# Causal blocks of 64 rows, two heads side by side in one score tile, other products in four bursts per slot

## The chip, the core and the metric

The program runs on one core of a Trainium2 chip. Its engines work at the same time and meet only at semaphores: the PE (TensorE, the matrix product, which loads a stationary operand, the weights, and streams a moving one past it into PSUM), DVE (VectorE), ACT (ScalarE), POOL (GpSimd) and SP (SyncE, here the one that issues all transfers). The metric is the time of one execution on the device in microseconds, as the median of several runs. A profile shows one such execution.

## What is computed

Each of 32 sequences of 256 rows and 128 columns is normalised by rows (xn). The result is x + attention(xn) + experts(xn):

```python
scores = jnp.einsum('bhqd,bhkd->bhqk', q, k) / math.sqrt(hd)
causal = jnp.tril(jnp.ones((s, s), bool))
scores = jnp.where(causal, scores, -jnp.inf)
attn = jax.nn.softmax(scores, axis=-1)
out = jnp.einsum('bhqk,bhkd->bhqd', attn, v)
out = out.transpose(0, 2, 1, 3).reshape(b, s, d)
return out @ Wo.T + bo
...
logits = jnp.einsum('btd,ed->bte', x, gate_w)
top_val, top_idx = jax.lax.top_k(logits, top_k)
top_w = jax.nn.softmax(top_val, axis=-1)
y_all = jnp.einsum('btd,edm->btem', x, We)
x_experts = jnp.take_along_axis(y_all, top_idx[..., None], axis=2)
out = jnp.sum(x_experts * top_w[..., None], axis=2)
```

There are 16 heads of 8 columns, and two of 8 experts are kept for each row. All products are wanted to single precision.

## The kernel before

q and k are each split into three bf16 parts and stacked, with a causal mask written as further rows, so that one bf16 product over up to 123 rows gives a masked score to single precision (qstack and kstack, made by way of DRAM). A score is computed twice. The first pass (score_item, tile score_ps) has queries in the partitions; DVE takes the negated row maximum (take_max, into negmax). The maxima are transposed (pe_mT), split in two bf16 parts (mT, on ACT and DVE) and loaded by SP into two more rows of qstack. The second pass (scoreT_item, tile scoreT_ps) has keys in the partitions and gives scores less the maximum, of which ACT takes the exponential (take_exp, into probs). The values (values) then multiply probs by vaug, which holds v and a column of ones for the sum, in four column tiles of 32, one head in each; the result oT_ps is copied by ACT (oT), transposed (pe_o), divided on DVE (rden, o_sb), transposed again (pe_oTn), copied by ACT (oTn) and multiplied by Wo (pe_y); DVE adds the rest and SP stores it.

A tile holds 512 columns. Only blocks on or below the diagonal are computed, in blocks of 128 rows: of four, three. So a pass has 12 items of 4 matmuls of 128 columns, 3 items for each group of 4 heads. score_ps and scoreT_ps have two buffers each: item n + 2 of a pass waits on the PE until DVE (or ACT) has done with item n.

The other products of the PE: turn_input (transposes of xn, from which ACT and DVE make xnT and its two halves, copy_input, halve_input, round_input), project (q and k of a later sequence, into m2, which part1 on ACT and take_rest on DVE read), values and gates (pe_vg, into m1, read by take_values on ACT), and experts (four products of 512 columns, three passes each, into m1 for DVE, lower_experts, and m2 for ACT, upper_experts).

The order is written out by hand. Each engine has a function slot(t, s), called once for each slot s by over_slots; in it a loop over the items n, with the pieces of other work placed at an n. In slot s the scores are of sequence s, the turned scores of s-1 and s-2 (behind, with LAG items between), the experts of s-1, the values and what follows of s-2, the projections of s+2, the input of s+3. Each engine works through its own list, so an instruction that waits holds up what stands behind it in that list. There are 34 slots. What stands around the change on ACT is this:

```python
if n == 6 and has(s, -2):
    act.wait_ge(pe_pv, upto(fin, per=NG))
    act.wait_ge(pe_o, upto(fin + (-1)))
    a.copy(oT[:].rearrange("p r t -> p (r t)"), oT_ps[:]).then_inc(act_oT, 1)
...
f, k = behind(t, s, n)
if f:
    take_exp(f, k)
```

## Time and profile before

| | |
|---|---|
| three runs | 515.61, 516.22, 518.01 us; median 516.22 |
| profiled execution | span 510.5 us from its first to its last instruction; its time with what lies around the span is not listed apart |
| PE busy | 477.8 us, 94% of the span, 6274 instructions |
| DVE busy | 420.7 us, 82%, 1111 instructions |
| ACT busy | 396.9 us, 78%, 1062 instructions |
| POOL busy | 345.9 us, 68%, 561 instructions |
| DMA | 67.8 MB, 133 GB/s |
| chain that ended last | PE 89%, DVE 3%, ACT 3%, DMA 2% |

A busy share is the union of the instructions' times on an engine. Matmuls overlap in their pipeline: one of 128 columns lasts some 0.22 us in the trace, but the next starts after a quarter of that, so what the PE spends on a group is read from the start of the group to the start of the next. In the rows of the timeline neighbours of one kind are merged, with their count (x4) and the time from the first's start to the last's end.

### The profile page before, as it was taken

What the parts mean: (1) busy time and instruction counts of PE and PEld (TensorE: products, weight loads), DVE (VectorE), ACT (ScalarE), POOL (GpSimd) and SP (SyncE); (2) the same over time, 40 slices, a digit from 0 to 9 for tenths busy, and PEclk for the clock granted to TensorE, in tenths of its full rate; (3) what the DMA queues carried; (4) which work ended last, traced back from release to release, by engine and by line L of the source; (5) the groups of instructions that cost most, each with busy time, mean ns of one, the idle gap of its engine ahead of it and who ended that gap; (6) DMA issues with size and microseconds to landing.
All of it is one profiled execution on the core that took longest, in us unless ns stands there. A gap on an engine that the chain in (4) does not pass through costs nothing.

```text
span 510.5 us, 17312 instructions
## 1 busy us (share of the span) xinstructions
PE 477.8 (94%) x6274; PEld 393.8 (77%) x6274; DVE 420.7 (82%) x1111; ACT 396.9 (78%) x1062; POOL 345.9 (68%) x561
## 2 busy tenths in 40 slices
PE   2548799999999999999999999999999999999995
PEld 1437688888888888888888888888888888888863
DVE  5897698888888898888888898888888898888721
ACT  3644688888888888888888888888888888887773
POOL 7264657777777777778777777777777777755443
PEclk9999999999999999999999999999999999999999
DMA  4664746656547566655465566655556566552000
GB/s 124 195 140 117 188 122 152 161 136 156 134 119 162 130 151 156 160 139 145 105 168 128 148 154 160 156 141 143 139 128 147 138 152 161 133 132 44 15 13 22
DMA packets 64281, 67.79 MB, mean 133 GB/s; under 512 B 6828, under 2 KB 59180, under 8 KB 59484
## 3 DMA queue, kind: packets, MB, share of 16 engines
q1 hardware_dynamic: 64196, 66.68, 53.0%
q8 instruction: 50, 0.82, 0.7%
q14 instruction: 35, 0.29, 0.2%
HBM read 44.90 MB, written 21.23 MB: 130 GB/s over the span
## 4 chain that ended last, share of the span: by engine, by line
PE 89%; DVE 3%; ACT 3%; DMA 2%; issue 2%; SPq 0%; POOL 0%; DVEq 0%; POOLq 0%; ACTq 0%
PE m L841 23%; PE oT_ps L911 17%; PE scoreT_ps L887 13%; PE score_ps L867 12%; PE scoreT_ps L892 5%; PE score_ps L861 5%; PE m L953 3%; PE m L996 3%; PE m L1014 3%; PE m L926 2%; PE m L1021 1%; PE m L962 1%; DMA qstack<-mT 1%; ACT probs L499 1%; DVE negmax L625 1%
## 5 line engine op out<-in xcount | busy, mean ns | idle before, releaser
L625 DVE TENSOR_REDUCE negmax<-score_ps 128x2 f32<-128x512 f32 (+1 forms) x384 | 249.7, 678 | 46.4 <-PE score_ps L867 43.7
L499 ACT ACTIVATE probs<-scoreT_ps 128x512 f32<-128x512 f32 x384 | 216.5, 603 | 74.2 <-PE scoreT_ps L887 48.0
L394 POOL TENSOR_TENSOR fours<-lower,upper 128x512 f32<-128x512 f32 x64 | 81.7, 1276 | 54.1 <-ACT upper L549 54.1
L841 PE MATMUL m<-we_hl,xnT_hl 128*128 128x512 f32 x384 | 114.6, 420 | 0.0
L867 PE MATMUL score_ps<-kstack,qstack 72*128 72x128 bf16 (+1 forms) x1024 | 103.8, 224 | 5.6 <-DVE negmax L625 5.5
L887 PE MATMUL scoreT_ps<-qstack,kstack 123*128 123x128 bf16 (+1 forms) x1024 | 102.0, 221 | 3.3 <-DMA qstack<-mT 2.6
L911 PE MATMUL oT_ps<-probs,vaug 128*32 128x256 f32 (+1 forms) x2048 | 96.7, 329 | 0.2 <-ACT probs L499 0.2
L887 PEld LDWEIGHTS scoreT_ps<-qstack,kstack 123*128 123x128 bf16 (+1 forms) x1024 | 68.1, 98 | 26.5 <-ACT probs L499 15.4
L911 PEld LDWEIGHTS oT_ps<-probs,vaug 128*32 128x32 f32 x2048 | 57.3, 109 | 29.1 <-ACT probs L499 0.4
L549 ACT ACTIVATE upper<-m,weight 128x128 f32<-128x128 f32 x256 | 73.1, 376 | 8.2 <-PE m L841 8.2
L867 PEld LDWEIGHTS score_ps<-kstack,qstack 72*128 72x128 bf16 (+1 forms) x1024 | 72.1, 100 | 8.8 <-DVE negmax L625 7.6
L841 PEld LDWEIGHTS m<-we_hl,xnT_hl 128*128 128x128 f32 x384 | 65.8, 192 | 8.9
L371 POOL TENSOR_TENSOR parts<-rest,parts 128x256 bf16<-128x256 f32 x60 | 40.1, 690 | 35.2 <-ACT parts L528 35.2
L861 PE MATMUL score_ps<-kstack,qstack 123*128 123x128 bf16 x512 | 51.1, 223 | 2.4 <-DVE negmax L625 1.4
L361 POOL TENSOR_SCALAR xn<-x_sb,mv,rstd 128x128 f32<-128x128 f32 x58 | 46.4, 806 | 7.4 <-POOL rstd L353 7.4
L892 PE MATMUL scoreT_ps<-qstack,kstack 123*128 123x128 bf16 x512 | 50.1, 220 | 0.7 <-ACT probs L499 0.7
L662 DVE TENSOR_TENSOR lower<-m,weight 128x512 f32<-128x512 f32 x64 | 43.5, 679 | 2.6 <-PE m L841 2.6
L433 POOL TENSOR_TENSOR pairs<-fours 128x512 f32<-128x512 f32 x32 | 40.7, 1272 | 2.5
L892 PEld LDWEIGHTS scoreT_ps<-qstack,kstack 123*128 123x128 bf16 x512 | 31.8, 98 | 11.2 <-issue 8.7
L861 PEld LDWEIGHTS score_ps<-kstack,qstack 123*128 123x128 bf16 x512 | 35.3, 99 | 3.3 <-DVE negmax L625 2.0
L841 PE MATMUL m<-xnT_hl,wqk_hl 128*128 128x256 f32 x192 | 33.3, 314 | 4.1 <-DVE xnT_hl L678 4.1
L841 PEld LDWEIGHTS m<-xnT_hl,wqk_hl 128*128 128x128 f32 x192 | 27.3, 207 | 5.6 <-issue 4.9
(81 smaller groups left out, 649.7 us busy)
## 6 DMA issues: line engine op xcount, KB each, us to landing
kstack<-scratch SPq DMA_DIRECT2D x93, 192.0 KB
scratch<-parts SPq DMA_DIRECT2D x64, 192.0 KB, 2.4
qstack<-scratch SPq DMA_DIRECT2D x62, 192.0 KB
qstack<-scratch SPq DMA_DIRECT2D x31, 256.0 KB
x_sb<-in_x SPq DMA_DIRECT2D x32, 128.0 KB, 2.3
scratch<-parts SPq DMA_DIRECT2D x32, 128.0 KB, 1.9
out<-out_sb SPq DMA_DIRECT2D x32, 128.0 KB, 3.7
qstack<-mT SPq DMA_DIRECT2D x64, 8.0 KB, 2.1
```

The source lines that it names most:

```text
L361: ins = g.tensor_scalar(xn[:, q, :], x_sb[nxt.buf][:, q, :], mv[:, q, 0:1], rstd[:, q:q + 1], ALU.subtract, ALU.mult)
L394: g.tensor_tensor(fours[:, :, q, :], lower[:, :, q, :], upper[:, :, q, :], ALU.add).then_inc(pool_sum, 1)
L499: a.activation(o, i, ACT.Exp, scale=SCALE).then_inc(act_exp, 1)
L549: ins = a.activation(upper[:, e, q, :], m2[:, e * D:(e + 1) * D], ACT.Copy, scale=weight[m.buf][:, q, EH + e:EH + e + 1])
L625: v.tensor_reduce(o, score_ps[n % 2][:].rearrange("p (h k) -> p h k", h=w), axis=AX.X, op=ALU.max, negate=True).then_inc(dve_max, 1)
L662: v.tensor_tensor(lower[:, :, q, :], m1[:].rearrange("p (e m) -> p e m", e=EH), weight[m.buf][:, q, 0:EH].unsqueeze(2).to_broadcast([P, EH ...
L841: ins = tn.matmul(o, l, r, start=first, stop=l is low)
L861: ins = tn.matmul(ps[:, c * P:(c + 1) * P], qs[0:ALL_ROWS, h, 0:P], ks[0:ALL_ROWS, h, 0:P], start=True, stop=True)
L867: ins = tn.matmul(ps[:, c * S + q * P:c * S + (q + 1) * P], qs[0:top, h, P:S], ks[0:top, h, q * P:(q + 1) * P], start=True, stop=True)
L887: ins = tn.matmul(ps[:, c * S + q * P:c * S + (q + 1) * P], ks[0:top, h, 0:P], qs[0:top, h, q * P:(q + 1) * P], start=True, stop=True)
L892: ins = tn.matmul(ps[:, c * P:(c + 1) * P], ks[0:ALL_ROWS, h, P:S], qs[0:ALL_ROWS, h, P:S], start=True, stop=True)
L911: ins = tn.matmul(o, va[:, q, h, :], i, start=q == 0 and grp % VGRP == 0, stop=q == 1 and grp % VGRP == VGRP - 1, skip_group_check=True)
```

## The change

Scores, turned scores and values go by blocks of 64 rows: of 16 blocks 10 lie on or below the diagonal. The array is used as two column tiles of 64: head h goes to PSUM partitions 0 to 63 and head h + 8 to 64 to 127 of the same tile, by two matmuls with stationary operands of 64 columns, one behind the other. An item of 512 columns then holds blocks of two or four such pairs. A pass has 10 items in two sets of five kinds: `low` (two pairs, three steps each of 64, 128 and 64 columns), `mid` (four pairs, one step of 128) and `top` (two pairs, two steps of 128). The row maxima of `low` items come out in parts, and a small reduction on DVE folds them (fold_max). vaug holds keys of two heads in the upper and lower partitions, with the two heads' values in different columns, so one matmul of the values serves both; the values come in two bursts of 16. Values and gates and the output product go in two column tiles too.

The order is new on all engines. On the PE the other products stand at four places of a slot: two transposes of o_sb, that of negmax, project and values and gates at n = 1; values and half the experts at n = 3; the same at n = 6; transposes of oT and of the input at n = 8. The end of a sequence (the second transposes, output product, store) moves a slot later, and there are 35 slots. The maxima's rows are loaded by four transfers and not two.

```diff
--- before.py
+++ after.py
...
-HG = 4
-NG = H // HG
-ITEMS = 3 * NG
+BLK = HALF
+NBLK = S // BLK
+NPAIR = H // 2
+SETS = 2
+QUADS = NPAIR // SETS
+KINDS = 5
+ITEMS = SETS * KINDS
...
+def score_tables():
+
+
+    low = [[(c, (c % 2) * S, 0, ALL_ROWS, 0, 1), (c, (c % 2) * S + BLK, 2, MAX_ROW, 0, 2),
+            (c, (c % 2) * S + 3 * BLK, 2, ALL_ROWS, 2, 3)] for c in range(QUADS)]
+    mid = [(c, c * P, 1, ALL_ROWS, 0, 2) for c in range(QUADS)]
+    top = [[(c, (c % 2) * S, 3, MAX_ROW, 0, 2), (c, (c % 2) * S + P, 3, ALL_ROWS, 2, 4)] for c in range(QUADS)]
+    return [low[0] + low[1], low[2] + low[3], mid, top[0] + top[1], top[2] + top[3]]
...
+    mid = [(c, c * P, 2, ALL_ROWS, 2, 4) for c in range(QUADS)]
...
+
+SCORES, SCORES_T = score_tables(), turned_tables()
+PROBS = {(c, blk): (kind, col) for c in range(QUADS) for blk, kind, col in
+         ((0, c // 2, (c % 2) * S), (1, 3 + c // 2, (c % 2) * S), (2, 2, c * P), (3, 3 + c // 2, (c % 2) * S + 3 * BLK))}
 
 
 def stand_alone(eng, passed):
...
                     m = t + (-1)
 
                     sp.wait_ge(dve_mT, upto(m))
                     for part in range(MAX_PARTS):
-                        sp.dma_start(qstack[m.buf][MAX_ROW + part:MAX_ROW + part + 1], mT[:, part]).then_inc(dma_max, 16)
+                        for half in range(2):
+                            row = qstack[m.buf][MAX_ROW + part:MAX_ROW + part + 1, half * NPAIR:(half + 1) * NPAIR]
+                            sp.dma_start(row.rearrange("r c (i t) -> r (c i) t", i=NBLK),
+                                         mT[:, part, half * HALF:(half + 1) * HALF]).then_inc(dma_max, 16)
                 if s == 1:
...
+                if has(s, -3):
+                    store(t + (-3))
...
-                pr = probs[grp]
+                group, kind = k // KINDS, k % KINDS
                 act.wait_ge(pe_scoreT, upto(f, per=ITEMS, k=k + 1))
...
-                    o = pr[:, 1]
-                    i = scoreT_ps[k % 2][:].rearrange("p (h q) -> p h q", h=HG)
-                a.activation(o, i, ACT.Exp, scale=SCALE).then_inc(act_exp, 1)
+                if kind == 0:
+                    act.wait_ge(pe_pv, upto(f + (-1), per=SETS, k=group + 1))
+                a.activation(probs[group][:, kind], scoreT_ps[k % 2][:], ACT.Exp, scale=SCALE).then_inc(act_exp, 1)
...
+                    f, k = behind(t, s, n)
+                    if n == 1 and has(s, -1):
+                        act.wait_ge(pe_mT, upto(mix))
+                        act.wait_ge(dma_max, upto(mix + (-1), per=MAX_LOADS, unit=16))
+                        a.copy(mT[:, 0], oT_ps[0:NPAIR * NBLK, 0:P]).then_inc(act_mT, 1)
...
-                    if n == 6 and has(s, -2):
-                        act.wait_ge(pe_pv, upto(fin, per=NG))
+                    if n == 3 and has(s, -3):
+                        act.wait_ge(pe_oTn, upto(last))
+                        act.wait_ge(pe_y, upto(last + (-1)))
+                        a.copy(oTn[:], m0[:, 0:S]).then_inc(act_oTn, 1)
+                    if n == 7 and has(s, -2):
+                        act.wait_ge(pe_pv, upto(fin, per=SETS))
                         act.wait_ge(pe_o, upto(fin + (-1)))
                         a.copy(oT[:].rearrange("p r t -> p (r t)"), oT_ps[:]).then_inc(act_oT, 1)
-                    if n == 11 and has(s, NXT):
-                        copy_input(t + NXT)
-                    if n == 11 and has(s, -1):
-                        upper_experts(mix, 1)
-                    if n == 11 and has(s, NXT):
-                        round_input(t + NXT)
-                    f, k = behind(t, s, n)
                     if f:
                         take_exp(f, k)
...
+                    if n in (4, 5) and has(s, -1):
+                        upper_experts(mix, 0, range(2 * (n - 4), 2 * (n - 3)))
+                    if n in (7, 8) and has(s, -1):
+                        upper_experts(mix, 1, range(2 * (n - 7), 2 * (n - 6)))
+                    if n == 8 and has(s, NXT):
+                        copy_input(t + NXT)
+                    if n == 9 and has(s, NXT):
+                        round_input(t + NXT)
...
+                nm, ps = negmax[t.buf], score_ps[n % 2][:]
+                first, kind = QUADS * (n // KINDS), n % KINDS
+                some = slice(first + 2 * (kind % 2), first + 2 * (kind % 2) + 2)
+                if kind < 2:
+                    o, i = nm[:, :, some, 0].rearrange("p g c -> p c g"), ps.rearrange("p (c g k) -> p c g k", c=2, g=NBLK)
+                elif kind == 2:
...
+            def fold_max(t):
+
+                nm = negmax[t.buf]
+                dve.wait_ge(dve_max, upto(t, per=ITEMS, k=KINDS + 2))
+                v.tensor_reduce(nm[:, 0, :, 2], nm[:, 1:NBLK, :, 0].rearrange("p g c -> p c g"),
+                                axis=AX.X, op=ALU.min).then_inc(dve_fold, 1)
...
+                    if n == 3 and has(s, 0):
+                        best_numbers(t)
+                    if n == 4 and has(s, -1):
+                        lower_experts(mix, 0)
...
+                    if n == 7 and has(s, -1):
+                        lower_experts(mix, 1)
+                    if n == 7 and has(s, 0):
+                        fold_max(t)
...
+                for pair, col, blk, top, k0, k1 in SCORES[n % KINDS]:
+                    for half in range(2):
+                        h = head(QUADS * (n // KINDS) + pair, half)
+                        ins = tn.matmul(ps[half * HALF:(half + 1) * HALF, col:col + (k1 - k0) * BLK],
+                                        qs[0:top, h, blk * BLK:(blk + 1) * BLK], ks[0:top, h, k0 * BLK:k1 * BLK],
                                         start=True, stop=True)
...
+                for pair, col, blk, top, q0, q1 in SCORES_T[n % KINDS]:
+                    for half in range(2):
+                        h = head(QUADS * (n // KINDS) + pair, half)
+                        ins = tn.matmul(ps[half * HALF:(half + 1) * HALF, col:col + (q1 - q0) * BLK],
+                                        ks[0:top, h, blk * BLK:(blk + 1) * BLK], qs[0:top, h, q0 * BLK:q1 * BLK],
                                         start=True, stop=True)
...
-                        o = oT_ps[quad, c0:c0 + S] if q == 0 else oT_ps[quad, c0 + P:c0 + S]
-                        i = pr[:, 0:3:2, c, :] if q == 0 else pr[:, 1, c, :]
-                        ins = tn.matmul(o, va[:, q, h, :], i, start=q == 0 and grp % VGRP == 0,
-                                        stop=q == 1 and grp % VGRP == VGRP - 1, skip_group_check=True)
+                    pe.wait_ge(dve_mT, upto(f + 1) if f.n + 1 < NSEQ else upto(f))
+                for blk in range(NBLK):
+                    for c in range(QUADS):
+                        kind, col = PROBS[c, blk]
+                        ins = tn.matmul(oT_ps[VW * c:VW * (c + 1), group * S + blk * BLK:(group + 1) * S],
+                                        vaug[f.buf][:, blk, QUADS * group + c, :],
+                                        probs[group][:, kind, col:col + S - blk * BLK],
+                                        start=blk == 0, stop=blk == NBLK - 1, skip_group_check=True)
...
+            def values_and_gates(t, s):
...
+                for blk in range(NBLK):
+                    for half in range(2):
+                        skip = 0 if blk % 2 == half else E
+                        ins = tn.matmul(m1[half * HALF:(half + 1) * HALF, blk * GV + skip:(blk + 1) * GV],
+                                        xnT[t.buf][:, blk * BLK:(blk + 1) * BLK], wvg_sb[:, half * GV + skip:(half + 1) * GV],
+                                        start=True, stop=True)
+                ins.then_inc(pe_vg, 1)
...
+                    if n == 1 and has(s, -3):
...
+                            ins = tn.transpose(m0[:, q * P:(q + 1) * P], o_sb[:, q].rearrange("p j c d -> p (j c d)"), ident[:])
+                        ins.then_inc(pe_oTn, 1)
...
+                        pe.wait_ge(dve_fold, upto(mix))
+                        pe.wait_ge(act_oT, upto(last))
+                        tn.transpose(oT_ps[0:NPAIR * NBLK, 0:P], negmax[mix.buf][:, 0].rearrange("p c i -> p (c i)"),
+                                     ident[:]).then_inc(pe_mT, 1)
                     if n == 1 and has(s, PRE):
...
+                    if n == 1 and has(s, 0):
+                        values_and_gates(t, s)
                     if n == 3 and has(s, -2):
                         values(fin, 0)
-                        values(fin, 1)
-                    if n == 4 and has(s, -1):
+                    if n == 3 and has(s, -1):
                         if s == 1:
...
-                        experts(mix, 1)
+                        mix_experts(mix, s, 0)
+                    if n == 4 and has(s, -3):
+                        pe.wait_ge(act_oTn, upto(last))
+                        for blk in range(NBLK):
+                            half = blk % 2
+                            ins = tn.matmul(m0[half * HALF:(half + 1) * HALF, blk // 2 * P:(blk // 2 + 1) * P],
+                                            oTn[:, blk * BLK:(blk + 1) * BLK], wo_sb[:], start=True, stop=True)
+                        ins.then_inc(pe_y, 1)
                     if n == 6 and has(s, -2):
-                        values(fin, 2)
-                        values(fin, 3)
+                        values(fin, 1)
+                    if n == 6 and has(s, -1):
+                        mix_experts(mix, s, 1)
...
-                    if n == 9 and has(s, -1):
-                        pe.wait_ge(dve_lower, upto(mix, per=2, k=1))
-                        experts(mix, 2)
-                    if n == 11 and has(s, NXT):
...
-                        ins.then_inc(pe_y, 1)
                     if f:
                         scoreT_item(f, k)
```

How the instructions stand now is shown at three places. score_ps and scoreT_ps are the two passes' tiles, m0 to m2 the PSUM tiles of the other products. The first is the PE from the end of the second values of a slot to the transposes of oT. Before:

```order
L911 MATMUL oT_ps<-probs3,vaug0 32x256 x4
L911 MATMUL oT_ps<-probs3,vaug0 32x128 x4
L887 MATMUL scoreT_ps1<-qstack1,kstack1 128x128 x4
L867 MATMUL score_ps1<-kstack2,qstack2 128x128 x4
L892 MATMUL scoreT_ps0<-qstack1,kstack1 128x128 x4
L867 MATMUL score_ps0<-kstack2,qstack2 128x128 x4
L996 MATMUL m0<-ident,oT 128x128 x4
L887 MATMUL scoreT_ps1<-qstack1,kstack1 128x128 x4
L861 MATMUL score_ps1<-kstack2,qstack2 128x128 x4
L841 MATMUL m1<-we_hl,xnT_hl1 128x512 x3
```

After:

```order
L939 MATMUL oT_ps<-probs1,vaug2 32x128 x4
L939 MATMUL oT_ps<-probs1,vaug2 32x64 x4
L885 MATMUL m1<-we_hl,xnT_hl3 128x512 x3
L885 MATMUL m2<-we_hl,xnT_hl3 128x512 x3
L923 MATMUL scoreT_ps1<-qstack3,kstack3 64x128 x8
L904 MATMUL score_ps1<-kstack0,qstack0 64x128 x8
L923 MATMUL scoreT_ps0<-qstack3,kstack3 64x128 x8
L904 MATMUL score_ps0<-kstack0,qstack0 64x128 x8
L1049 MATMUL m0<-ident,oT 128x128 x4
L956 MATMUL m1<-ident,xn 128x128 x2
L923 MATMUL scoreT_ps1<-qstack3,kstack3 64x64 x2
L923 MATMUL scoreT_ps1<-qstack3,kstack3 64x128 x2
```

Four items (turned score, score, turned score, score) stand ahead of the transposes of oT as before, but now six matmuls of the experts stand between the values and the first of them. The second place is ACT at the same point of the slot. Before:

```order
L499 ACTIVATE probs0<-scoreT_ps0 128x2x2x128 [waits pe_pv,pe_scoreT]
L549 ACTIVATE upper<-m2,weight2 128x128 [waits pool_sum,pool_gate,pe_moe]
L549 ACTIVATE upper<-m2,weight2 128x128 x3
L567 COPY oT<-oT_ps 128x512 [waits pe_o,pe_pv]
L499 ACTIVATE probs0<-scoreT_ps1 128x2x2x128 [waits pe_scoreT]
L499 ACTIVATE probs0<-scoreT_ps0 128x512 [waits pe_scoreT]
L499 ACTIVATE probs1<-scoreT_ps1 128x2x2x128 [waits pe_pv,pe_scoreT]
```

After:

```order
L581 ACTIVATE upper<-m2,weight2 128x128 x2
L530 ACTIVATE probs0<-scoreT_ps1 128x512 [waits pe_scoreT]
L605 COPY oT<-oT_ps 128x512 [waits pe_o,pe_pv]
L530 ACTIVATE probs0<-scoreT_ps0 128x512 [waits pe_scoreT]
L581 ACTIVATE upper<-m2,weight2 128x128 [waits pool_sum,pool_gate,pe_moe]
L581 ACTIVATE upper<-m2,weight2 128x128
L530 ACTIVATE probs0<-scoreT_ps1 128x512 [waits pe_scoreT]
L581 ACTIVATE upper<-m2,weight2 128x128 x2
L568 COPY xnT2<-m1 128x256 [waits pe_xnT]
L530 ACTIVATE probs0<-scoreT_ps0 128x512 [waits pe_scoreT]
L573 CAST xnT_hl2<-xnT_high 128x256 [waits pe_moe,dve_halves]
L530 ACTIVATE probs1<-scoreT_ps1 128x512 [waits pe_pv,pe_scoreT]
```

The copy of oT stood ahead of the first exponential of the items that follow the values on the PE; now it stands behind it. The third place is the PE at the start of a slot, where project takes the halves of the input. Before:

```order
L887 MATMUL scoreT_ps1<-qstack1,kstack1 128x128 x4
L867 MATMUL score_ps1<-kstack3,qstack3 128x128 x4
L953 MATMUL m1<-wvg_sb,xnT3 128x136 x2
L962 MATMUL m0<-ident,negmax2 16x128 x2
L841 MATMUL m2<-xnT_hl1,wqk_hl 128x256 x6
L892 MATMUL scoreT_ps0<-qstack1,kstack1 128x128 x4
```

After:

```order
L904 MATMUL score_ps1<-kstack0,qstack0 64x64 x2
L1010 MATMUL m0<-ident,o_sb 128x128 x2
L1016 MATMUL oT_ps<-ident,negmax3 32x128
L885 MATMUL m2<-xnT_hl2,wqk_hl 128x256 x6
L979 MATMUL m1<-wvg_sb,xnT0 64x72
L979 MATMUL m1<-wvg_sb,xnT0 64x64 x2
L979 MATMUL m1<-wvg_sb,xnT0 64x72 x2
L979 MATMUL m1<-wvg_sb,xnT0 64x64 x2
L979 MATMUL m1<-wvg_sb,xnT0 64x72
L923 MATMUL scoreT_ps0<-qstack2,kstack2 64x128 x8
```

project has moved ahead of values and gates, and the second transposes (of o_sb) have come in front of it.

## Rows read from the trace of the kernel before

**Rows 1.** By stretch, twenty slots: us; busy us and count by engine; clock; DMA.
```profile
106.17:394.01 287.84, 287.84 (x3919) 240.94 (x3917) 252.67 (x680) 240.41 (x660) 213.09 (x341) 1.00 0.59 145
```

**Rows 2.** Waits of the PE, longest first: us in total, times, longest; first and last.
```profile
PE m L926 <- DVE xn L781: 8.2, 3, 6.2
...
PE m L996 <- ACT oT L567: 1.2, 2, 0.7
...
PE oT_ps L911 <- ACT probs L499: 0.2, 1, 0.2
```

**Rows 3.** Timeline, PE: start, us, engine, line, operation, tiles, count; a burst of values.
```profile
250.22 0.39 PE L887 MATMUL scoreT_ps<-qstack,kstack 123*128 123x128 bf16 x4
...
250.45 0.39 PE L861 MATMUL score_ps<-kstack,qstack 123*128 123x128 bf16 x4
...
250.77 1.51 PE L911 MATMUL oT_ps<-probs,vaug 128*32 128x256 f32 x32
...
252.21 0.41 PE L887 MATMUL scoreT_ps<-qstack,kstack 123*128 123x128 bf16 x4
```

**Rows 4.** By stretch, instructions on oT_ps alone: PE, PEld, ACT; clock; DMA.
```profile
250.70:250.80 0.10, 0.03 (x4) 0.03 (x5) 0.00 (x0) 1.00 0.95 251
```

**Rows 5.** Timeline, PE: the other products of a slot, with the groups behind them.
```profile
253.14 0.60 PE L996 MATMUL m<-ident,oT 128*128 128x128 f32 x4
...
253.59 0.40 PE L887 MATMUL scoreT_ps<-qstack,kstack 123*128 123x128 bf16 x4
...
258.30 0.68 PE L953 MATMUL m<-wvg_sb,xnT 128*128 128x136 f32 x4
...
258.82 0.38 PE L962 MATMUL m<-ident,negmax 128*16 128x128 f32 x2
...
258.95 0.96 PE L841 MATMUL m<-xnT_hl,wqk_hl 128*128 128x256 f32 x6
...
259.75 0.40 PE L892 MATMUL scoreT_ps<-qstack,kstack 123*128 123x128 bf16 x4
...
262.66 1.65 PE L841 MATMUL m<-we_hl,xnT_hl 128*128 128x512 f32 x6
...
264.14 0.40 PE L892 MATMUL scoreT_ps<-qstack,kstack 123*128 123x128 bf16 x4
```

**Rows 6.** Timeline: ACT, SP, and the two PE groups ahead of the third.
```profile
251.16 1.14 ACT L549 ACTIVATE upper<-m,weight 128x128 f32<-128x128 f32 x4
...
254.81 0.40 PE L887 MATMUL scoreT_ps<-qstack,kstack 123*128 123x128 bf16 x4
...
255.05 0.39 PE L867 MATMUL score_ps<-kstack,qstack 72*128 72x128 bf16 x4
...
255.25 1.09 ACT L499 ACTIVATE probs<-scoreT_ps 128x512 f32<-128x512 f32 x2 [0.63 <-PE scoreT_ps L887]
...
256.47 0.41 ACT L537 COPY xnT<-m 128x256 f32<-128x256 f32 x1
...
260.60 1.86 SPq L318 DMA_DIRECT2D qstack<-mT  x2
260.68 0.83 ACT L522 ACTIVATE parts<-m,bqk_sb 128x256 bf16<-128x256 f32 x2
...
263.15 0.70 ACT L528 CAST parts<-rest 128x256 bf16<-128x256 f32 x2
```

**Rows 7.** Timeline, DVE: the halves of the input, and rest.
```profile
257.02 0.42 DVE L674 TENSOR_SCALAR xnT_high<-m 128x256 uint32<-128x256 uint32 x1
...
257.47 0.42 DVE L678 TENSOR_TENSOR xnT_hl<-m,xnT_high 128x256 fp32r<-128x256 f32 x1
...
261.55 0.88 DVE L716 SCALAR_TENSOR_TENSOR rest<-m,bqk_sb,parts 128x256 f32<-128x256 f32 x2
```

**Rows 8.** Timeline, end of the program: a copy on ACT and who waited for it.
```profile
503.99 0.58 ACT L567 COPY oT<-oT_ps 128x512 f32<-128x512 f32 x1 [0.98 <-PE oT_ps L911]
...
504.63 0.66 PE L996 MATMUL m<-ident,oT 128*128 128x128 f32 x4 [0.71 <-ACT oT L567]
```

294 lines of the change are left out of this document (117 added, 177 removed).

## The prediction

> **What bounds the kernel now.** The first view is the table by stretches over twenty slots of the middle (a slot is one turn of the program's loop, on average one sequence). 287.84 us for twenty is 14.39 us a slot, and the PE is busy in all of it at the full granted clock of 1.00, while DVE works 12.63 us of a slot (252.67/20) and ACT 12.02 [rows 1]. Busy alone proves little for a pipelined engine, so the second view is the PE's waits: over the whole run they come to some 30 us in 14 rows, the longest from the start of the program, and the row that matters below, the PE waiting for ACT's copy of oT, stands there twice in 34 slots, 1.2 us together [rows 2]. So the PE never waits in the middle, and a slot lasts as long as the PE's stream of instructions. Work taken off DVE and ACT is worth nothing by itself. The third view is the PE's line of time, where the start of one group to the start of the next is its price: a score item of four matmuls of 128 columns costs 0.23 us, 0.058 a matmul (250.22 to 250.45) [rows 3].
>
> **What the change takes from the PE.** I write S0 to S9 and T0 to T9 for the new score and turned-score items (12 of each become 10).
> Scores: 96 matmuls of 128 columns (24 items, 5.5 us) become 96 steps of two matmuls each, one for each half of the array: 64 steps of 128 columns, 32 of 64. Do two column tiles run at the same time? In before the values run in four column tiles: four matmuls start inside a tenth of a microsecond, with at least as many weight loads [rows 4], so I take yes. A step of 128 columns then stays at 0.058. A step of 64 columns lies between its own columns, 0.033, and a weight load that hides no more: 128 columns of weights are loaded within a step of 0.11 (four steps in 0.45, 253.14 to 253.59) [rows 5], so 64 take at most about 0.058. I take 0.033, since in the nearest row, the values, the loads of a column tile hide behind the matmuls, and keep 0.058 for the range. Scores: 64 x 0.058 + 32 x 0.033 = 4.8 us, -0.7 (at 0.058: 5.6, no gain).
> The Trainium skill speaks against the change here: "TensorEngine Tiling (Array Packing)", Restrictions, says that column tiling switches Fast Weight Load off, and "TensorE: Matmul & The Clock Gate", LDWEIGHTS, puts a load without it at columns/1.2 ns, by which I estimate 53 ns for 64 columns. By that the upper end would hold, and the slot below would be 15.9 us, not 15.7; no row of before has a bf16 load in a column tile.
> Values: a burst of 32 instructions covers 768 columns (two groups of heads, 384 each) in each of four tiles and costs 1.44 us until the next group [rows 3]; a burst of one group in blocks of 64 covers 640. Less 0.10 for the way out, 1.34 x 5/6 = 1.12 us, twice a slot: -0.4.
> Between tilings the array seems to run empty: the item ahead of the values costs 0.32 and not 0.23 (250.45 to 250.77) [rows 3], so about 0.09 on the way in, and I take 0.10 on the way out. Before there are four such borders in a slot; now there are ten (one full-width burst ahead of the gates, values and experts twice, the transposes of oT and of the input). Six more: +0.6. Against it, the transposes of negmax, also in a 32-wide tile, follow full-width products with no gap (258.82, next 258.95) [rows 5], so zero is the lower bound.
> The Trainium skill states the same of a border ("TensorEngine Tiling", Key Properties: a change of mode drains the TensorE); the values agree, the negmax rows do not.
> The rest is equal within 0.1: experts 1.48 for six (262.66 to 264.14, less in two bursts of six than in three), project 0.80, values and gates 0.52, transposes of oT 0.45, each to the start of the next group [rows 5]; the output product, in half-width tiles, I put at 0.45 like these, one transpose of negmax at 0.1 where two stood.
> The PE's own sum: 4.8 + 2.24 + 2.96 + 0.80 + 0.53 + 0.45 + 0.45 + 0.23 + 0.22 + 0.1 + ten borders 0.96 = 13.7 us, 0.7 less than now.
>
> **What it adds: waits.** The other products now stand in four bursts. While the PE is in one, ACT and DVE run out of scores (each has two PSUM tiles); afterwards the PE waits for what they queued behind the next item. Prices: a score item on the PE reaches ACT 0.20 after the next group starts (255.05 to 255.25); two exponentials take 1.09, four experts' weightings 1.14, so two hold ACT 0.50, and I put the two vaug copies, of the same columns in all, at 0.52; two part1 take 0.83, part2 0.30 each [rows 6]. DVE: high to low 0.45, low 0.42; two rest 0.88 [rows 7]. ACT's copy of oT, of 512 columns like an exponential, lasts 0.58, and the PE starts 0.06 after its end (504.57 to 504.63) [rows 8]; so I take 0.58 for one exponential and 0.51 until ACT goes on. I go around one slot, from the end of T3; six-step items are 0.25 (four short steps), four-step items 0.23.
> A. The next project needs the input's halves. ACT: 0.20, exponential of T3 0.51, two weightings 0.50, copy of xnT 0.41 + 0.06; DVE: high 0.45, low 0.42 + 0.06: 2.61. The PE's S9, T4, S0, T5, S1, a border, three transposes: 1.6. It waits 1.0.
> B. project 0.80, border 0.10, gates 0.53: 4.04.
> C. The second half of the first experts' burst writes m2, which project filled, after rest has read it: 0.20 + logits 0.1 + vaug 0.52 + exponential 0.51 + part1 0.89 + rest 0.94 = 3.16, against 3.03 on the PE (T6, S2, T7, S3, border, values, border, three experts' matmuls): 7.20.
> D. Three matmuls 0.74, border, T8 0.25: 8.29.
> E. The second values need the exponential of T9, behind that of T8 and part2: 0.20 + 0.51 + 0.60 + 0.1 + 0.64 = 2.05, against 1.75 on the PE (S4, output, T9, S5, T0, S6): 10.34.
> F. values 1.12, experts 1.48, two borders, T1 0.23: 13.37.
> G. The transposes of oT need ACT's copy. It now stands behind the exponential of T1, an item that comes after the burst; in before it stood ahead of the next exponential. 0.20 + 0.51 + 0.58 + 0.06 = 1.35, against S7, T2, S8 and a border, 0.78: 14.72. It waits 0.57.
> H. oT 0.45, input 0.22, border, T3 0.25: 15.74.
> So the slot is 15.7 us: 13.7 of work and 2.0 of waits in four places. That DVE has two reductions and ACT two exponentials less hides nothing of it: both idle during the bursts. SP issues four loads of the maxima where two took 1.86 us from the first issue [rows 6]; T0 wants them some 5 us after they are asked for, so twice that is still hidden; without this cover T0 would wait for it. The store of a result, now last in SP's slot, has a whole slot until out_sb is written again. The loop has one turn more, with the last sequence's end alone, which before stood in the turn ahead of it: nothing, +-2 us.
>
> **The sum.** 32 slots with scores x (15.74 - 14.39) = 43.2 us. The profiled execution's span is 510.5; the median of the runs, 516.22, is 5.7 more, which lies outside the span and stays. 516.2 + 43.2 = 559.4 us.
>
> **Rivals.**
> 1. Faster: the waits do not come and the PE's own 13.7 us is the slot. For it: the same waits stand in before and cost nothing [rows 2]. Against: the prices that the walk rests on [rows 6 to 8], which exceed the PE's cover by 0.3 to 1.0. It is decided at G and A: if oT is ready within 0.8 us of T1. 516.2 - 32 x 0.69 = 494. Chance 0.10.
> 2. No border costs anything, as with negmax. Five of them lie on the way round (B, D, two in F, H): 15.24, 516.2 + 27 = 543.4. Chance 0.17.
> 3. Steps cost more, 0.07 each whatever their columns (loads a little in the way): items 0.42 and 0.28; A and G still wait, D to F and H lengthen, to a slot of 16.4: 582. Chance 0.13.
> 4. The change does not do what it says: the two halves take turns, 0.11 a step. 96 x 0.11 = 10.6 and the rest 8.9 leave 19.5 us a slot, 680. Against it: the four matmuls inside a tenth of a microsecond [rows 4]. Chance 0.06.
> 5. No change within 0.5%, which is about what a measurement of this kernel can tell (2.6 us): waits and savings would have to balance by accident. 0.04.
>
> **How the numbers follow.** The forecast, 550 to 574 with the dearer short step inside (15.9, 566), has 0.50. Eight in ten then needs rivals 2 and 3: 538 to 584. Faster by over 0.5% is rival 1, 0.10; the same rival 5, 0.04; slower 0.86.
>
> **What would show it.** Right: a slot of 15.5 to 16.0; PE rows waiting for ACT oT, DVE xnT_hl, DVE rest and ACT probs, nearly 32 times each, about 0.6, 1.0, 0.1 and 0.3 us; DVE and ACT busy less than now, not more; a four-step item still 0.23, a six-step item 0.25 (0.35 if loads bind). Wrong: no such waits (rival 1); values following items at once (rival 2); two tiles' matmuls one behind the other (rival 4). Not priced: POOL's normalising, which must end before the input's transposes in H; if it is late, H is longer.

## The result, and the profile after

The changed kernel takes 588.7 us (median of four runs, 586.6 to 590.5), the kernel before 516.9 beside it: 1.139 times as long, 95% interval 1.136 to 1.143. Slower was forecast, with 559.4 us and a range to 584; the time lies 5 us above the range.

The regular slot, from the start of one project to the start of the next, lasts 16.71 us (14.39 before, 15.74 forecast), and in the rest of the text "slot" means this. Six slots by stretch in the changed kernel, as in [rows 1] (us; busy us and count of PE, PEld, DVE, ACT, POOL; granted clock; DMA share; GB/s):

```profile
330.35:430.60 100.25, 89.26 (x1842) 68.07 (x1843) 71.71 (x211) 68.92 (x193) 63.98 (x103) 1.00 0.51 129
```

The PE, which never paused in [rows 1], is now busy 14.9 of 16.7 us, at the same clock. DVE and ACT work less per slot than before (11.95 and 11.49 us, against 12.63 and 12.02), so neither has become the bound by its load. The waits of the PE in the changed kernel (total us, times, longest), where [rows 2] had next to nothing:

```profile
PE m L885 <- DVE xnT_hl L719: 21.8, 30, 2.8
...
PE m L1049 <- ACT oT L605: 16.2, 32, 0.9
...
PE m L885 <- DVE rest L757: 10.6, 23, 0.5
...
PE oT_ps L939 <- ACT probs L530: 7.5, 28, 0.7
```

These are the four waits of the walk, A, G, C and E. One slot on the PE's line of time in the changed kernel (start, us, engine, line, operation, tiles, count, idle before), against [rows 3] and [rows 5]:

```profile
321.04 0.40 PE L923 MATMUL scoreT_ps<-qstack,kstack 123*64 123x128 bf16 x8
321.27 0.41 PE L904 MATMUL score_ps<-kstack,qstack 123*64 123x64 bf16 x12
321.93 1.29 PE L939 MATMUL oT_ps<-probs,vaug 128*32 128x256 f32 x32 [0.25 <-ACT probs L530]
323.16 1.66 PE L885 MATMUL m<-we_hl,xnT_hl 128*128 128x512 f32 x6
324.74 0.42 PE L923 MATMUL scoreT_ps<-qstack,kstack 123*64 123x128 bf16 x8
325.00 0.39 PE L904 MATMUL score_ps<-kstack,qstack 123*64 123x128 bf16 x8
...
325.45 0.40 PE L904 MATMUL score_ps<-kstack,qstack 72*64 72x128 bf16 x8
326.33 0.66 PE L1049 MATMUL m<-ident,oT 128*128 128x128 f32 x4 [0.49 <-ACT oT L605]
326.99 0.41 PE L956 MATMUL m<-ident,xn 128*128 128x128 f32 x2
327.33 0.43 PE L923 MATMUL scoreT_ps<-qstack,kstack 123*64 123x64 bf16 x12
327.60 0.40 PE L904 MATMUL score_ps<-kstack,qstack 72*64 72x128 bf16 x8
...
329.45 0.27 PE L1016 MATMUL oT_ps<-ident,negmax 128*32 128x128 f32 x1
330.35 0.94 PE L885 MATMUL m<-xnT_hl,wqk_hl 128*128 128x256 f32 x6 [0.63 <-DVE xnT_hl L719]
331.23 0.70 PE L979 MATMUL m<-wvg_sb,xnT 128*64 128x72 f32 x16
331.76 0.41 PE L923 MATMUL scoreT_ps<-qstack,kstack 123*64 123x128 bf16 x8
...
332.44 0.41 PE L904 MATMUL score_ps<-kstack,qstack 72*64 72x128 bf16 x8
332.78 1.29 PE L939 MATMUL oT_ps<-probs,vaug 128*32 128x256 f32 x32
...
335.43 0.74 PE L885 MATMUL m<-we_hl,xnT_hl 128*128 128x512 f32 x2 [0.46 <-DVE rest L757]
```

An item of eight matmuls of 128 columns costs 0.22 to 0.26 (332.00 to 332.22, 324.74 to 325.00), about what four such matmuls cost before (0.23): the two halves of the array do run together. An item of twelve costs 0.24 to 0.27 (327.33 to 327.60). On ACT, against [rows 6], the copies behind the gates are long, and the copy of oT stands behind an exponential:

```profile
325.21 0.60 ACT L530 ACTIVATE probs<-scoreT_ps 128x512 f32<-128x512 f32 x1 [1.81 <-PE scoreT_ps L923]
325.70 0.58 ACT L605 COPY oT<-oT_ps 128x512 f32<-128x512 f32 x1
...
331.98 0.34 ACT L537 COPY logits<-m 64x16 f32<-64x16 f32 x2 [1.26 <-PE m L979]
332.33 0.78 ACT L544 COPY vaug<-m 64x256 f32<-64x256 f32 x2
333.14 0.60 ACT L530 ACTIVATE probs<-scoreT_ps 128x512 f32<-128x512 f32 x1
...
334.83 0.39 ACT L601 COPY oTn<-m 128x256 f32<-128x256 f32 x1
```

ACT stands idle ahead of both groups (1.81, 1.26), then the PE waits for it: that is what a burst costs. Not foreseen at all were a few stops of the PE that the profile puts down to no releaser. One of them in the changed kernel:

```profile
432.47 0.40 PE L923 MATMUL scoreT_ps<-qstack,kstack 123*64 123x128 bf16 x8
432.69 0.35 PE L904 MATMUL score_ps<-kstack,qstack 72*64 72x128 bf16 x6
434.68 0.25 PE L904 MATMUL score_ps<-kstack,qstack 123*64 123x128 bf16 x2 [1.64 <-issue]
```

The PE stops in the middle of an item, which waits for nothing. There are five stops of 1.0 to 1.7 us from 230 us on.

### The profile page after: what moved, and what is told of

Read it like the earlier page. It is cut to its first block, busy times and chain, and to the rows that moved or that the text cites. A ratio compares the mean times of both kernels' runs of the same rounds, so it can differ in the third digit from the quotient of the medians.

```text
span 586.7 us, 24454 instructions
## 1 busy us (share of the span) xinstructions
PE 492.2 (84%) x9826; PEld 374.7 (64%) x9826; DVE 397.8 (68%) x1143; ACT 380.6 (65%) x1030; POOL 347.2 (59%) x565
## 4 chain that ended last, share of the span: by engine, by line
PE 48%; ACT 24%; issue 13%; DVE 9%; DMA 2%; SPq 1%; POOL 1%; ACTq 0%; DVEq 0%; POOLq 0%
PE m L885 20%; PE oT_ps L939 9%; ACT probs L530 8%; PE scoreT_ps L923 7%; PE m L979 4%; PE m L1049 4%; ACT oT L605 3%; ACT parts L553 3%; ACT upper L581 3%; DVE rest L757 2%; ACT parts L559 2%; DVE xnT_high L715 2%; DVE xnT_hl L719 2%; PE score_ps L904 2%; PE m L956 2%
## 5 line engine op out<-in xcount | busy, mean ns | idle before, releaser
L662 DVE TENSOR_REDUCE negmax<-score_ps 128x8 f32<-128x512 f32 (+2 forms) x320 | 216.3, 685 | 111.3 <-PE score_ps L904 111.0
L530 ACT ACTIVATE probs<-scoreT_ps 128x512 f32<-128x512 f32 x320 | 192.0, 603 | 135.2 <-PE scoreT_ps L923 133.8
L904 PE MATMUL score_ps<-kstack,qstack 123*64 123x64 bf16 (+2 forms) x3072 | 132.4, 216 | 11.3 <-DVE negmax L662 6.8
L923 PE MATMUL scoreT_ps<-qstack,kstack 123*64 123x128 bf16 (+2 forms) x3072 | 131.8, 214 | 3.4 <-DMA qstack<-mT 2.7
L923 PEld LDWEIGHTS scoreT_ps<-qstack,kstack 123*64 123x64 bf16 (+1 forms) x3072 | 94.0, 110 | 36.5 <-issue 27.8
L904 PEld LDWEIGHTS score_ps<-kstack,qstack 123*64 123x64 bf16 (+1 forms) x3072 | 95.3, 113 | 16.5 <-DVE negmax L662 8.3
L939 PE MATMUL oT_ps<-probs,vaug 128*32 128x256 f32 (+3 forms) x2048 | 84.8, 304 | 12.7 <-ACT probs L530 7.5
L757 DVE SCALAR_TENSOR_TENSOR rest<-m,bqk_sb,parts 128x256 f32<-128x256 f32 x64 | 28.0, 479 | 27.9 <-ACT parts L553 27.9
L483 POOL TENSOR_TENSOR res<-mixed,xb 128x256 f32<-128x256 f32 x32 | 23.4, 732 | 27.2 <-DVE out_sb L796 27.2
L537 ACT COPY logits<-m 64x16 f32<-64x16 f32 x64 | 10.7, 167 | 42.7 <-PE m L979 42.3
```

The costliest lines, as they stand in the source:

```text
L530: a.activation(probs[group][:, kind], scoreT_ps[k % 2][:], ACT.Exp, scale=SCALE).then_inc(act_exp, 1)
L662: v.tensor_reduce(o, i, axis=AX.X, op=ALU.max, negate=True).then_inc(dve_max, 1)
L904: ins = tn.matmul(ps[half * HALF:(half + 1) * HALF, col:col + (k1 - k0) * BLK], qs[0:top, h, blk * BLK:(blk + 1) * BLK], ks[0:top, h, k0 * ...
L923: ins = tn.matmul(ps[half * HALF:(half + 1) * HALF, col:col + (q1 - q0) * BLK], ks[0:top, h, blk * BLK:(blk + 1) * BLK], qs[0:top, h, q0 * ...
L939: ins = tn.matmul(oT_ps[VW * c:VW * (c + 1), group * S + blk * BLK:(group + 1) * S], vaug[f.buf][:, blk, QUADS * group + c, :], probs[grou ...
```

## The four waits, one at a time

Is the slot one chain around the engines, so that a wait that is removed comes off it, or is the PE's own stream the bound? For each wait, one kernel makes the work that it waits for earlier. The quoted paragraph behind each edit was put on record before that kernel ran. e1_oT_first, on ACT (G):

```diff
-                    if n == 7 and has(s, -2):
+                    if n == 6 and has(s, -2):
                         act.wait_ge(pe_pv, upto(fin, per=SETS))
```

> The changed kernel, with one thing undone: ACT's copy of oT stands ahead of the exponential of T1 again, as before the change. In the changed kernel the regular slot is 16.71 us, of which the PE idles 0.49 ahead of the transposes of oT. Theory 'waits' (the slot is one chain round PE, ACT and DVE, and a wait that is removed comes off it): the slot falls by the wait, to 16.2, and the whole by 32 x 0.49, some 16 us. Theory 'POOL next' (what the prediction left unpriced): POOL's xn ends at 326.85 in the changed kernel, 0.14 before the PE reaches the input's transposes at 326.99; with oT earlier the PE waits there for POOL, and the slot falls by 0.1 alone, to 16.6, 3 to 4 us in all, with a new PE wait on xn of about 0.4 a slot. Theory 'PE bound' (the short steps, borders and loads set the slot, the waits are slack): 16.7, no change. I expect POOL next.

The slot stayed at 16.71. The transposes of oT and of the input in this kernel:

```profile
311.91 0.66 PE L1049 MATMUL m<-ident,oT 128*128 128x128 f32 x4
...
313.12 0.41 PE L956 MATMUL m<-ident,xn 128*128 128x128 f32 x2 [0.56 <-POOL xn L400]
```

The wait for oT is gone, and 0.56 us of waiting for POOL's xn stands behind it: "POOL next", and the whole gain went there. The time, 593.9, is above the changed kernel's, with more and longer stops (below). e2_oT_and_norm adds, on POOL:

```diff
-                    if n == 5 and has(s, NXT):
-                        normalise(t + NXT)
...
+                    if n == 4 and has(s, NXT):
+                        normalise(t + NXT)
                     if n == 4 and has(s, PRE):
                         part3(t + PRE)
```

> As e1_oT_first, and POOL normalises the next input ahead of its third parts of q and k instead of behind them and behind res (POOL idles 4.9 us there in the changed kernel). Theories 'waits' and 'POOL next' agree here: both the oT wait and the xn wait are gone, slot 16.2, some 16 us less in all than the changed kernel (571 to 573). 'PE bound': 16.7 and no change.

Slot 16.51, 579.1 us: 0.20 gained where 0.5 was expected, since the next late work stood right behind, DVE's lower, which must have read m1 before the input's transposes write it:

```profile
PE m L956 <- DVE lower L705: 10.2, 28, 0.9
```

e3_halves (A): on ACT copy_input and round_input move ahead of take_exp of the same n, on the PE the transposes of o_sb behind values_and_gates, and on DVE

```diff
+                    if n == 9 and has(s, NXT):
+                        halve_input(t + NXT, s)
                     if n == 9 and has(s, -2):
...
-                    if n == 9 and has(s, NXT):
-                        halve_input(t + NXT, s)
```

> The changed kernel, with the way of the input's halves shortened: ACT copies xnT and rounds its high half ahead of the exponentials of the same item, DVE makes the halves ahead of o_sb, and the PE takes the two transposes of o_sb behind the gates. Theory 'waits': DVE's reduction of S9 ends 0.56 before its high half starts in the changed kernel, so project starts about 0.55 earlier: slot 16.15, PE's wait for the halves under 0.15, some 17 us less in all. Theory 'DVE full' (DVE's work between rden and project is what binds, in whatever order): the o_sb products come later, the PE waits for them behind the gates or for the reductions instead, slot 16.5 to 16.7. 'PE bound': 16.7.

Slot 16.13, 581.4 us: -0.58, the number of the waits' theory, but not by its way. It wanted under 0.15 us a slot of waiting for the halves; the wait fell only from 0.63 to some 0.34 (13.7 us in all). The rest came from C: the wait for rest vanished too, probably since the o_sb products behind the gates give ACT and DVE that time, and there the number was luck. e4_logits (C):

```diff
                     if n == 2 and has(s, PRE):
                         part1(t + PRE)
+                    if n == 2 and has(s, 0):
+                        take_values(t, s)
...
+            def take_logits(t):
+                dve.wait_ge(pe_vg, upto(t))
...
+                    ins = v.tensor_copy(logits[lanes], m1[lanes, 0:NBLK * GV].rearrange("p (i c) -> p i c", c=GV)[:, half::2, 0:E])
+                ins.then_inc(dve_logits, 1)
```

> The changed kernel, with the way from the gates to rest shortened: DVE and not ACT copies the logits, and ACT copies vaug behind the exponential of T6 and part1 instead of ahead of them. In the changed kernel ACT has logits 0.35 and vaug 0.78 there, where I had put 0.62 together; the PE waits 0.46 for rest inside the first experts. Theory 'waits': that wait goes (under 0.1), slot 16.25, some 15 us less in all. 'PE bound' or a new wait of the same size for the vaug copies ahead of the first experts' products: 16.7.

Slot 16.19, 576.2 us: -0.52, as expected; 0.2 us of waiting for the vaug copies are new. e5_part2 (E), with POOL's edit of e2_oT_and_norm:

```diff
-                    if n == 3 and has(s, PRE):
+                    if n == 4 and has(s, PRE):
                         part2(t + PRE)
```

> The changed kernel, with ACT's part2 behind the exponential of T9 instead of ahead of it, and POOL's normalising ahead of its third parts so that POOL does not become late by it. Theory 'waits': the PE's wait for probs ahead of the second values (0.25 idle, 0.32 with the pipeline's end) goes, slot 16.4, some 10 us less in all. Theory 'PE bound': 16.7.

Slot 16.46, 582.1 us: -0.25. So "PE bound" falls: the waits of C and E come off the slot whole when removed alone, that of A in part and together with C's, that of G only as far as the next late engine lets it.

## All together, and the PE's own sum

> The edits of e2_oT_and_norm, e3_halves, e4_logits and e5_part2 together. The first three took 0.21, 0.58 and 0.52 off the regular slot. Theory 'waits': they lie at different places of the one chain and add up, with e5 to 16.71 - 1.6 = 15.1 at most, and less if DVE's lower, for which the PE waits in e2_oT_and_norm ahead of the input's transposes, is the only wait left: the PE's own groups of the changed kernel, each to the start of the next without a wait, add up to 14.1. So 14.5 to 15.1. Rival 'one engine full' (ACT or DVE has no more room round the bursts): it stays above 15.5, since each edit only moves work between them.

Slot 15.89, 563.4 us: -0.82, not the -1.55 that the single gains add up to. The rival's number held (above 15.5), and the gains do not add up, in part because e3_halves and e4_logits had removed the same wait for rest: in e6_all the PE waits for lower again (10.2 us in all), for the halves (13.6) and for vaug (5.3). e7_all_lower also has, on DVE,

```diff
+                    if n == 7 and has(s, -1):
+                        lower_experts(mix, 1)
                     if has(s, 0):
                         take_max(t, n)
```

> e6_all, and on DVE the second lower ahead of the reduction of S7 instead of behind it (DVE idles 1.4 us there in the changed kernel). Theory 'waits': the last large wait goes, and what is left is the PE's own sum, 14.1 to 14.5 a slot where the kernel before has 14.39: the new blocks and bursts save the PE at most 0.3, not the 0.7 of my sum. In all 512 to 525, the upper part if stalls of the PE without a releaser stay, so no better than the kernel before. Rival of my prediction's own sum: 13.7 a slot and 500.

547.35 us, 1.062 times the kernel before (1.058 to 1.067), slot 15.32 where nothing disturbs it (15.5 on average from the sixth on). So neither engine was full in e6_all: one step moved on DVE took another 0.57 off. The order alone thus costs 1.4 of the 2.3 us that a slot has grown, but 14.1 to 14.5 was missed. What was left was either the PE's own work or ACT and DVE around the bursts, which e12_light separates, by halving the columns of the exponentials and of the score items' reductions and leaving out the other half:

```diff
-            a.activation(probs[group][:, kind], scoreT_ps[k % 2][:], ACT.Exp, scale=SCALE).then_inc(act_exp, 1)
+            some = 2 * S if f.n == 0 else S
+            a.activation(probs[group][:, kind, 0:some], scoreT_ps[k % 2][:, 0:some], ACT.Exp, scale=SCALE).then_inc(act_exp, 1)
...
-                v.tensor_reduce(o, i, axis=AX.X, op=ALU.max, negate=True).then_inc(dve_max, 1)
+                v.tensor_reduce(o, i[..., 0:i.shape[-1] // 2], axis=AX.X, op=ALU.max, negate=True).then_inc(dve_max, 1)
```

> e7_all_lower with the short loads of e11, and with the exponentials (from the second sequence on) and the reductions of the score items taken over half of their columns, so that ACT and DVE have some 20 half-length instructions a slot each; the PE's work is all there. It measures the PE's own sum of the changed blocks and bursts, which I predicted as 13.7 us a slot. Theory 'own sum 14.1' (from the groups of the changed kernel, each to the start of the next where nothing waits): 14.1 to 14.4 a slot; e7's waits (project 0.5, vaug 0.3, the items ahead of project 0.4) mostly gone. My prediction's sum: 13.7. Rival 'not DVE and ACT': it stays at 15.3 because something else, POOL or the chain of short steps, sets e7's slot.

Slot 14.57, 515.9 us, a little above the 14.1 to 14.4 expected. So ACT and DVE held e7_all_lower up by 0.75 a slot, although in 15 us of it (first row) DVE works 11.47 and ACT 10.71. (The short loads, which e12_light has too, left the regular slot of the changed kernel at 16.7 in e11_short_loads, below; in e7_all_lower they were not tried alone.) Behind it one slot of e12_light by stretch, where the PE still idles 0.34, and then its line of time around project:

```profile
160.00:175.00 15.00, 14.48 (x313) 11.46 (x310) 11.47 (x36) 10.71 (x30) 10.75 (x17) 1.00 0.59 140
```

```profile
300.97:315.54 14.57, 14.23 (x309) 11.43 (x308) 9.53 (x38) 9.29 (x30) 10.72 (x18) 1.00 0.20 58
```

```profile
302.00 0.66 PE L1060 MATMUL m<-ident,oT 128*128 128x128 f32 x4
302.50 0.38 PE L966 MATMUL m<-ident,xn 128*128 128x128 f32 x2
...
304.37 0.28 PE L1022 MATMUL oT_ps<-ident,negmax 128*32 128x128 f32 x1
304.99 0.93 PE L895 MATMUL m<-xnT_hl,wqk_hl 128*128 128x256 f32 x6 [0.34 <-DVE xnT_hl L727]
305.85 0.70 PE L989 MATMUL m<-wvg_sb,xnT 128*64 128x72 f32 x16
306.49 0.44 PE L1032 MATMUL m<-ident,o_sb 128*128 128x128 f32 x2
306.85 0.42 PE L933 MATMUL scoreT_ps<-qstack,kstack 123*64 123x128 bf16 x8
```

One wait is left: from negmax's transpose, taken at 0.13 like the two in [rows 5], to project the PE loses 0.49. Without it the PE's own stream is 14.1 us. In this order the o_sb products are a burst of their own, with two more borders (the gates cost 0.64 instead of 0.53, the two products 0.36 instead of 0.27), so I estimate 13.9 for the changed kernel's own order, where I had 13.7; the kernel before has 14.39.

## The stops

The stops of the changed kernel come at matmuls 3493, 5007, 7152, 8413 and 9046 of the PE's list. e1_oT_first and e3_halves, with a list of the same length, stop for 0.9 us or more at the same five and at two more (1349 and 2232); here is the one at 7152 in e1_oT_first, between the sixth and seventh matmul of the same item, but a microsecond longer:

```profile
437.06 0.35 PE L904 MATMUL score_ps<-kstack,qstack 72*64 72x128 bf16 x6
440.15 0.25 PE L904 MATMUL score_ps<-kstack,qstack 123*64 123x128 bf16 x2 [2.75 <-issue]
```

e2_oT_and_norm and e5_part2, whose edits leave the PE's list as it is, stop that long at 1349 and 8413 alone, and at 2232, 3493, 8413 and 9046: the places belong to the list, but whether the PE stops there, and how long, does not. e4_logits, which adds waits to the list, stops at others (1347, 4117, 6259, 9031). One DMA queue, q8, carries instructions in packets of 16 KB, and their number goes with the PE's matmuls: 50 in the kernel before (6274), 78 now (9826). Is the length of the list enough? e8_before_in_two changes the kernel before:

```diff
+            def in_two(ps, col, still, moving, first):
+                for c in (0, P // 2):
+                    ins = tn.matmul(ps[:, col + c:col + c + P // 2], still, moving[:, first + c:first + c + P // 2],
+                                    start=True, stop=True)
+                return ins
```

> The kernel before, with each score matmul of 128 columns written as two of 64 with the same weights (96 more matmuls a slot, 9346 in all instead of 6274; the changed kernel has 9826). Two questions. Stalls: in the changed kernel and in e1 and e3 the PE stops for 1 to 3.5 us at the same matmuls of its list (numbers 490, 3493, 5007, 7152, 8413, 9046), in e4, whose list differs, at others, each time with a fetch of 16 KB of instructions landing in the stop. Theory 'list': with a list half as long again the kernel before gets such stops too, 4 to 8 of them of 1 to 3 us. Theory 'blocks' (something in the column tiles or in the data's transfers stops it): none. Steps: if the load of 128 columns of weights does not hide behind 64 columns, the slot grows, by up to 96 x 0.05 = 5 us; if it does, the slot stays at 14.4.

74 packets on q8, and no stop in a regular slot: "list" alone falls. Twenty slots of it:

```profile
200.00:494.00 294.00, 294.00 (x5874) 249.49 (x5874) 250.06 (x663) 238.32 (x653) 207.98 (x331) 1.00 0.55 135
```

14.70 a slot, 0.3 more for 96 more matmuls, and the PE never idle: here a load of 128 columns hides behind 64 moving ones but for 0.003 us each. Next, the loads of the stacks: e9_split_loads and e10_all_split issue each in two halves.

```diff
+            def load_twice(pre):
+                for pairs in (slice(0, QUADS), slice(QUADS, NPAIR)):
+                    load_stacks(pre, pairs, dma_stack[pre.buf])
```

> The changed kernel, with each sequence's load of qstack and kstack from DRAM issued as two times six transfers of half the heads (4 KB rows) instead of six of all (8 KB rows). e8_before_in_two has shown that a longer list alone does not stop the PE: no stop in its regular slots. In the trace of the changed kernel the fetches of the PE's instructions that end a stop (230.1, 314.3, 432.3, 501.4, 535.2) each begin within 0.5 us of the end of such a load, which lasts 7 us, some 12 us after the fetch before instead of 7. Theory 'queue' (a fetch that falls due while the load runs waits for a gap in it, and the PE eats up its list): with more and shorter transfers there are more gaps, the stops of over 0.8 us go or fall to one or two, the regular slot stays at 16.7, and the whole falls by 4 to 8 us, to 580 to 585. Rival 'place' (the stops belong to places of the list whatever the transfers do): the same stops at the same matmuls, 588.

> e7_all_lower with the loads split as in e9_split_loads. Theory 'queue': e7's slots that last over 15.35 (15.5 to 16.75, some 14 of 27) go back to 15.3, 4 to 6 us less: 541 to 544. Rival 'place': 547. In either case it stays slower than the kernel before by about 27 us, 32 slots of 15.3 against 14.39.

638.6 and 629.2 us: both forecasts missed by far, for a reason of its own. SP now issues twelve loads a slot at 0.7 to 1.0 us each (six at 0.4 in the changed kernel), the maxima's rows stand behind them in its list, and T0 waits, in e9_split_loads

```profile
PE scoreT_ps L927 <- DMA qstack<-mT: 46.1, 18, 6.8
```

PE rows without a releaser are gone in both, but so many other waits may give the fetches time, so this decides nothing. e11_short_loads keeps the six transfers and makes them short:

```diff
-                    n = PART_ROWS + (ZERO_ROWS if r == PARTS - 1 else 0)
+                    n = PART_ROWS + (ZERO_ROWS if r == PARTS - 1 else 0) if pre.n < NB else 1
```

> e9_split_loads gave other waits (SP issues twelve transfers a slot, and the maxima's rows come late behind them), so it did not decide. Here the changed kernel keeps its six transfers, but from the fifth sequence on each brings one row a head and not 24 to 32, so the stacks' loads nearly vanish (all other rows of q and k stay those of the first four sequences, the work of all engines stays). Theory 'queue' (a fetch of the PE's instructions that falls due while the 7 us load runs waits for its end): the stops without a releaser (231.0, 315.1, 433.0, 502.3 and 536.8 in the changed kernel) are gone, every regular slot is 16.7, and the whole falls by 4 to 8 us, to 580 to 585. Rival 'place' (the stops belong to places of the PE's list): the same stops at matmuls 3493, 5007, 7152, 8413 and 9046.

All 26 slots from the sixth on are 16.68 to 16.75, none of the five stops is there, and the time is 581.6, 7.1 less than the changed kernel's. "Queue" holds: the loads make the stops. In the changed kernel, the queues from 306 to 314.2 us, while a load runs, and from 314.2 to 315.4, behind its end (queue, kind: packets, MB, share of 16 engines):

```profile
q1 hardware_dynamic: 487, 1.37, 75.8%
```

```profile
q8 instruction: 1, 0.02, 5.2%
q1 hardware_dynamic: 61, 0.01, 4.3%
```

No fetch starts while this load runs, one starts as it ends, at 314.26, and from 315.12 to 316.81 the PE stands still. The other four stops look the same, a fetch at the end of a load that had none in its middle. But not every load holds a fetch back, in the changed kernel either: one starts at 345.5 in the load from 342.2 to 349, and the PE does not stop. Why a fetch gets into the middle of one load and not of another, and in e8_before_in_two (one at 237.0, in a load from 232.5 to 240.8) often enough that nothing stops, stays open.

## Why the prediction was wrong

The direction, the cause and the places were right; two terms of the walk were too small, and one cost was not in it. The walk, step by step, forecast and measured (from 327.60, the end of T3, around to the next):

| step | forecast | measured |
|---|---|---|
| A, to the start of project | 2.61 | 2.75 |
| B, project and gates | 1.43 | 1.41 |
| C, to the second half of the first experts | 3.16 | 3.67 |
| D, to the end of T8 | 1.09 | 1.16 |
| E, to the second values | 2.05 | 2.05 |
| F, to the end of T1 | 3.03 | 3.07 |
| G, to the transposes of oT | 1.35 | 1.33 |
| H, to the end of T3 | 1.02 | 1.27 |
| slot | 15.74 | 16.71 |

**C is the step that failed.** I priced logits 0.1, and the two vaug copies 0.52, "of the same columns in all" as two weightings. They are not. In the kernel before they were copies over all 128 partitions:

```profile
259.41 0.20 ACT L504 COPY logits<-m 128x16 f32<-128x16 f32 x1
259.46 0.50 ACT L514 COPY vaug<-m 128x128 f32<-128x128 f32 x2
```

Now each half of the partitions has its own copy, so logits are two copies (331.98 to 332.33, 0.35) and each vaug copy has 64 partitions and 256 columns, not 128 and 128 (332.33 to 333.14, 0.81). ACT's time here goes by columns, not by elements: a copy of 64x256 takes 0.39, one of 128x256 the same (oTn, 334.83), one of 128x128 0.25. 1.16 in place of 0.62 is 0.54, less 0.03 elsewhere the 0.51 of the row, 16 us over 32 slots, and e4_logits took 0.52 back.

**H:** I took the transposes of oT at 0.45, their price behind other products of the PE [rows 5]. Behind a wait they cost 0.66 (326.33 to 326.99), in e12_light without the wait 0.50; the rest is 0.34 for the input's with their border (0.32 forecast) and 0.27 for T3 (0.25). **A** is 0.14 more, but not for late halves:

```profile
329.21 0.42 DVE L715 TENSOR_SCALAR xnT_high<-m 128x256 uint32<-128x256 uint32 x1
329.67 0.42 DVE L719 TENSOR_TENSOR xnT_hl<-m,xnT_high 128x256 fp32r<-128x256 f32 x1
```

The high half starts 0.07 earlier than the walk had it (1.61 behind the end of T3, not 1.68), but project starts 0.26 behind the end of the low half (330.09 to 330.35), where I had 0.06; why, no run tells.

**The PE's own sum** was close (13.9 against 13.7). The twenty items cost 5.17 in e12_light, 4.73 less four borders ahead of other products (4.8 forecast). A step of 64 columns costs some 0.035: a six-step item (two steps of 128 columns, 0.11, and four short ones) takes 0.25. So the dear short step, 0.058, falls. The Trainium skill ("TensorEngine Tiling (Array Packing)", Restrictions: column tiling switches Fast Weight Load off) spoke for it; the items do not agree, the loads stay hidden, and no run shows whether that mode is off. Borders cost 0.12 on the way in (the item ahead of the values takes 0.34, 332.44 to 332.78, its like 0.22) and 0.11 on the way out (from the last values, 322.99, to the next product, 323.16, 0.17, where such steps of 64 columns follow each other by 0.06). Rival 2 falls: what the Trainium skill says of a change of mode ("TensorEngine Tiling (Array Packing)", Key Properties: it drains the TensorE) agrees with these rows in that a change takes time. Rival 1 (no waits), rival 4 (halves in turn) and rival 5 fall with the waits and the items above; rival 3's 582 is near the time, but its step of 0.07 is not there.

**POOL**, left unpriced: xn was ready 0.14 us before the PE wanted it, so it cost nothing here, but it ate the whole gain of G in e1_oT_first.

**The sum.** 0.97 more a slot is 31.0 us for 32 slots. The four stops in the regular slots add 4.7 (17.88 + 18.28 + 17.87 + 17.54 less four times 16.71). The first five slots and the tail grew by 11.6, not by six times 2.32, which takes 2.3, and what lies outside the span is 2.0 and not 5.7, which takes 3.7 (in the runs of the kernel before that list both it is 2.1 too: the profiled execution of 510.5 was a faster one than the median of the runs): 29.7 of the 29.3 that 588.7 stands above 559.4. The range failed to hold the time because each price of ACT was taken as a point and not between bounds, and because the stops had no place in it: without C's 16 us the time would lie inside it, at 572, without the four stops at its edge, at 584.

## What to carry to other kernels

Before products of the PE are gathered into bursts, walk the cycle around all engines once: work taken off every engine does not help when each burst lets ACT and DVE run dry and the next one waits for what they then do in a row. If a wait is removed, ask at once which engine is late next by how much, since here a whole wait of 0.49 us moved to POOL. When a copy is split over halves of the partitions, price it by its columns.

## What the hardware showed that was not expected

The PE's instructions come over the same DMA engines as the data (the profile counts q1 and q8 on the same 16), and with bulk loads of 7 us a fetch can come so late that the PE stops, for 1 to 2.75 us; it needs a fetch every 7.5 us on average here (78 in 587 us) and needed one every 10 before (50 in 511). The stop can cost twice: after one of 2.46 us in e4_logits the granted clock fell, by stretch (the stop, and the 6.8 us behind it)

```profile
372.80:375.30 2.50, 0.04 (x3) 0.01 (x2) 1.29 (x7) 1.01 (x3) 0.33 (x1) 0.89 0.20 44
375.30:382.10 6.80, 6.80 (x88) 5.43 (x92) 2.48 (x5) 2.50 (x8) 1.29 (x2) 0.54 0.13 38
```

to 0.54, that is to 1.2 GHz for most of the stretch, and that slot lasted 20.99 us; behind the stops of up to 1.7 us in the changed kernel it stayed at 1.00 (316.81 to 323.00). The length of the stop alone does not tell: over the 10 us behind stops of 2.15 and 2.75 us in e1_oT_first and of 2.77 in e3_halves (165.3) it was 0.83, behind one of 2.13 in e4_logits (526.1) and one of 2.40 in e3_halves (115.5) it stayed at 1.00.
